# Two stages of row-wise work in a graph network: table rows added by TensorE, small layer-norm operations for pairs of groups

## The chip, the cores and the metric

The kernel runs on one core of one Trainium2 chip, in fp32. The metric is the device time of one execution in microseconds. Three executions of the kernel before took 2436.28, 2438.08 and 2440.83 us (median 2438.08).

## The reference

50000 nodes have 160 features, 64 scalars and 32 vectors of 3; 25000 edges join them. Two layers of message passing are computed, each followed by a residual and a layer norm over the 160 features of a node:

```python
x = _layernorm(x + _L0_gnn_ref(x, node_vec1, src, dst, edge_attr_4, edge_attr_64, ...))
x = _layernorm(x + _L1_gnn_ref(x, node_vec1, edge_attr_16, edge_attr_4, src, dst, ...))
```

What the first layer does with a node, once the messages of its edges have been summed and mapped (`o_s`, `o_v`), is this:

```python
pre_s = sc_s + o_s          # sc_s = s @ sc_ws * a * inv : the self-connection, 96 columns
pre_v = sc_v + o_v          # sc_v : the same for the vectors, 3 x 32 columns
scalars = silu(pre_s[:, :64])
gates = sigmoid(pre_s[:, 64:96])
gated = gates[:, :, None] * pre_v
```

The layer norm is `(x - mean) / sqrt(var + 1e-5)`.

## The kernel before

The work has four stages, one after the other: edges of layer 0, nodes of layer 0, edges of layer 1, nodes of layer 1. The two edge stages run over 98 pairs of 128-edge tiles (gather rows of the source nodes, compute messages, sum those with the same destination, scatter-add them to a table in HBM). The two node stages run over NG = 98 groups of T = 4 tiles of 128 nodes. The change lies in the node stages.

Every engine has its own instruction stream, written out by hand. `run_stages` (L56) writes a software pipeline: in its step k an engine runs a list of pairs (lag, function), each function for group k - lag, in the order of the list. Buffers are rings of four (index u = g mod 4) or of two. Engines meet only in semaphores that count groups; `wait_count(engine, semaphore, n)` waits for a count of n, and engines execute in order, so that whatever stands behind a wait waits too. In functions, g is the count of groups from which the counts of the waits are made (it goes on from 98 in the second node stage).

The first node stage does this with group g:

- SP loads the turned features (`load_turned`, L374, two DMAs `xT` and `zT`) and the rows of the summed messages (`load_table`, L387, tile `tab`, 384 KB).
- TensorE: `nodes0` (L608) multiplies the features with the self-connection's weights into PSUM (`n0_ps`, two buffers; L603 for four tiles of 160 columns, L605 for the rest); `turn_back` (L614) turns the features back into rows in PSUM (`x0_ps`, `z0_ps`) for the residual.
- DVE: `add_table` (L896) adds PSUM and the table's rows into `tab`, which frees the PSUM buffer.
- ACT: `gates` (L715) takes the sigmoid of the first 96 columns, in four instructions.
- GpSimd: `scale_gates` (L499) multiplies them with the node's attribute.
- DVE: `gated0` (L903), two products into `res` (ring of four; it waits until group g - 4 has been normalised, `s_y`); `residual0` (L911), two additions from PSUM; `stats_of` (L947), four `bn_stats`.
- GpSimd: `powers` (L463) makes `rstd` and `shift` of the group from the statistics: eleven instructions on 128 x 4 elements with waits for its own results between them, `pow` at L483.
- ACT: `normalise` (L738), four activations of 160 columns with scale and bias per partition into `y`; `store` (L747) issues the DMA to HBM.

The order in a step of each engine, before:

```python
# TensorE                                                      L642
run_stages(pe, 0, NG, 6, [(0, nodes0), (1, turn_back)])
# ACT                                                          L755
[(0, gates)] ... + [(5, store), (4, normalise)]
# GpSimd                                                       L506
run_stages(pool, 0, NG, 10, [(0, scale_gates), (3, powers)])
# DVE                                                          L956
run_stages(dve, 0, NG, 6, [(2, gated0), (0, add_table), (2, residual0), (3, stats_of)])
```

The second node stage has the same tail: GpSimd runs `factor` (L487, three small operations for a group's mean over edges) and `powers` with lag 1 (L508); DVE runs `residual1` (L918), `stats_of` with lag 1 and `table_row1` (L939, which needs `factor`'s result) (L958); TensorE turns the features (`turn1`) and multiplies (`nodes1`) through `self_connection` (L600), which both stages share; ACT copies from PSUM and normalises as in the first (L755).

## Time and profile before

| what | value |
| --- | --- |
| median of 3 runs | 2438.08 us |
| runs | 2436.28 to 2440.83 us |
| profiled execution: span from first to last instruction | 2446.7 us |
| profiled execution: its own timer | not shown |
| PE / DVE / ACT / GpSimd busy, share of span | 71% / 62% / 44% / 72% |
| first node stage (L901, first to last start) | 867.5 to 1280.4 us |
| second node stage (L944, first to last start) | 2024.2 to 2434.8 us |
| TensorE's mean granted clock | 0.837 |

The span is that of one profiled execution, the times are of others. PE is TensorE, POOL GpSimd, SP the engine that issues loads; PEld is TensorE's loading of weights, which overlaps its matmuls. The granted clock is a share of 2.4 GHz: 0.5 is the lower level, 1.2 GHz. Each fp32 matmul of the code stands in the trace as two records, each transpose as one. In a timeline a row with xN is N instructions of one line that follow each other, from the start of the first to the end of the last; the ends of matmuls are modelled.

### The profile page before, as it was taken

To read this page: it belongs to the slowest core of one execution; us is meant where nothing else is said; L and a number is where in the kernel's file an instruction comes from. 1 tells how busy PE (TensorE), PEld (TensorE's weight loads), DVE (VectorE), ACT (ScalarE), POOL (GpSimd) and SP (SyncE) were. 2 spreads that over 40 slices of the span, in tenths; PEclk is the share of its full clock that TensorE was granted. 3 is DMA by queue.
4 is the path that set the end of the run, shared out by engine and by line. 5 is a ranking of instruction groups with operands and counts; after the bars stand their busy time and mean duration, and the time that the engine had idled before them with its cause. 6 is when DMAs were issued, how large, how long until landed. Compare 5 with 4: busy or idle time off the path is not lost. (4 is left out here: it accounts for less than half of the span.)

```text
span 2446.7 us, 50266 instructions
## 1 busy us (share of the span) xinstructions
PE 1726.5 (71%) x10412; PEld 1528.8 (62%) x10412; DVE 1506.3 (62%) x6121; ACT 1070.8 (44%) x3336; POOL 1751.4 (72%) x3148
## 2 busy tenths in 40 slices
PE   0478888888888666666665878678777766666664
PEld 0367776777776566666664767567666655556564
DVE  1266666666666468888883444444444427888886
ACT  0233333333333246666663333333333325566665
POOL 1066677766667568888884777777777757888887
PEclk9988889888888788888875888988798878878877
DMA  5975555555555467777772444444444436666664
GB/s 223 422 198 121 117 117 117 119 117 116 118 118 119 77 202 252 240 244 243 240 221 69 71 67 69 70 70 69 69 68 69 70 53 226 234 232 235 230 236 175
DMA packets 270387, 374.52 MB, mean 153 GB/s; under 512 B 62544, under 2 KB 172944, under 8 KB 267280
## 3 DMA queue, kind: packets, MB, share of 16 engines
q1 hardware_dynamic: 163264, 203.38, 28.8%
q0 software_dynamic: 75264, 67.79, 19.3%
q10 hardware_dynamic: 31824, 102.97, 10.4%
q8 instruction: 11, 0.18, 0.0%
q14 instruction: 24, 0.20, 0.0%
HBM read 202.83 MB, written 171.16 MB: 153 GB/s over the span
## 5 line engine op out<-in xcount | busy, mean ns | idle before, releaser
L453 POOL DMA_INDIRECT table<-sums,row_i x392 | 632.9, 1615 | 307.0 <-ACT sums L710 104.1
L743 ACT ACTIVATE y<-res,shift,rstd 128x160 f32<-128x160 f32 x784 | 343.8, 509 | 307.4 <-POOL shift L485 307.3
L695 ACT COPY msg<-ps 128x192 f32<-128x192 f32 (+1 forms) x196 | 57.4, 293 | 620.3 <-PE ps L592 437.1
L438 POOL DMA_INDIRECT xg<-in_x_rows,src_i x196 | 199.3, 1017 | 172.2 <-DMA src_i<-in_src_col 69.7
L603 PE MATMUL ps<-self_m,xT 128*128 128x160 f32 (+1 forms) x1568 | 303.8, 350 | 7.6 <-DVE tab L901 4.6
L526 PE MATMUL ps<-ident,xg 128*128 128x128 f32 x392 | 94.1, 325 | 293.1 <-ACT xz L682 214.8
L603 PEld LDWEIGHTS ps<-self_m,xT 128*128 128x128 f32 x1568 | 266.7, 239 | 17.2 <-issue 5.3
L526 PEld LDWEIGHTS ps<-ident,xg 128*128 128x128 f32 x392 | 42.3, 151 | 353.6 <-ACT xz L682 194.4
L438 POOL DMA_INDIRECT xg<-x_rows,src_i x196 | 195.5, 997 | 70.8 <-issue 62.9
L573 PE MATMUL ps<-mapA,midT 128*128 128x128 f32 (+1 forms) x784 | 189.1, 329 | 50.3 <-DVE msg L848 47.8
L483 POOL TENSOR_TENSOR rstd<-var_e,minus_half 128x4 f32<-128x4 f32 x196 | 203.7, 1039 | 15.4
L952 DVE BATCH_NORM_STATS2 stats<-res 128x6 f32<-128x160 f32 x784 | 194.8, 308 | 6.1 <-POOL shift L485 6.0
L573 PEld LDWEIGHTS ps<-mapA,midT 128*128 128x128 f32 x784 | 145.2, 231 | 72.1 <-issue 64.4
L807 DVE TENSOR_TENSOR prod<-hs,ea_all 128x192 f32<-128x192 f32 x196 | 70.2, 358 | 184.5 <-ACT hs L670 163.3
L575 PE MATMUL ps<-mapB,midT 128*128 128x96 f32 x784 | 177.4, 315 | 0.0
L627 PE MATMUL ps<-ident,x1g 128*128 128x128 f32 x392 | 74.9, 322 | 141.6 <-ACT x1z L729 133.7
L618 PE MATMUL ps<-ident,xT 128*128 128x128 f32 x392 | 73.7, 317 | 139.1 <-DVE res L916 138.9
L944 DVE SCALAR_TENSOR_TENSOR res<-tab,small,res 128x160 f32<-128x160 f32 x392 | 124.6, 379 | 69.8 <-POOL small L497 69.7
L886 DVE COPY row_i<-row_all 128x2 int32 (+1 forms) x98 | 17.5, 178 | 237.0 <-DMA table<-sums,row_i 234.9
L559 PE MATMUL ps<-ident,mid 128*128 128x128 f32 x784 | 154.9, 334 | 0.0
L575 PEld LDWEIGHTS ps<-mapB,midT 128*128 128x128 f32 x784 | 150.2, 238 | 0.0
L627 PEld LDWEIGHTS ps<-ident,x1g 128*128 128x128 f32 x392 | 48.5, 160 | 156.9 <-ACT x1z L729 105.6
(121 smaller groups left out, 5019.8 us busy)
## 6 DMA issues: line engine op xcount, KB each, us to landing
...
dst_row<-in_dst_row SPq DMA_DIRECT2D x196, 128.0 KB
```

What stands on the lines that cost most here:

```text
L438: pool.indirect_dma_start(out=xg[u][:, t, 0:width], out_offset=None, in_=rows, in_offset=bass.IndirectOffsetOnAxis(ap=src_i[u][:, t:t + 1] ...
L453: pool.indirect_dma_start(out=table[l], out_offset=bass.IndirectOffsetOnAxis(ap=row_i[u][:, t:t + 1], axis=0), in_=sums[u][:, t, 0:W], in_ ...
L483: tt(rstd[u][:, :], var_e[:, :], minus_half[:, :], ALU.pow).then_inc(s_rstd, 1)
L526: turn(xgT_ps[:, t, :], xg[u][:, t, 0:M], ident[:, :])
L559: last = turn(midT_ps[:, 2 * c + t, :], mid[u][:, t, c * P:(c + 1) * P], ident[:, :])
L573: mm(o_ps[l][:, t, 0:SO + V], midT[u][:, t, :], mapA[l][:, :], start=t == 0, stop=not L["cross"], skip_group_check=True)
L575: last = mm(o_ps[l][:, t, SO + V:SO + 4 * V], midT[u][:, 2 + t, :], mapB[l][:, :], start=False, stop=not L["cross"], skip_group_check=True)
L603: mm(o[:, t // 2, t % 2, 0:z], xT[u][:, t * P:(t + 1) * P], w_m[:, :], start=True, stop=True)
L627: turn(x1T_ps[u][:, t * P:(t + 1) * P], x1g[u][:, t, 0:M], ident[:, :])
L743: last = nc.scalar.activation(y[u][:, t, :], res[u][:, t, :], ACT.Identity, scale=rstd[u][:, t:t + 1], bias=shift[u][:, t:t + 1])
L944: last = stt(res[u][:, t, :], tab1[u][:, t, 1:161], small[u][:, t, 3:4], res[u][:, t, :], ALU.mult, ALU.add)
L952: last = nc.vector.bn_stats(stats[u][:, t, :], res[u][:, t, :])
```

## The change

In the first node stage TensorE adds the table's rows: `nodes0` accumulates identity times `tab` (four matmuls of 192 columns) on top of the self-connection in PSUM, and `add_table` is gone. ACT's sigmoid and DVE's products read PSUM in place of `tab`, and `nodes0` waits for `s_f` (the products of group g - 2) in place of `s_added`. The turned features come in one DMA into one tile; the z part is turned back by two transposes into the same PSUM rows as x, and the residual is one addition. `load_table` is released by `s_np`. DVE's order in a step and its lags change, TensorE's too.

In both node stages `powers` runs for two groups at once, when the second has its statistics, on 128 x 8 elements (ten instructions; no product with 0.25, a doubling of rstd in its place), and the fourth tile of each group is normalised by GpSimd (`normalise_last`), which `store` and the next user of `res` wait for (`s_y3`).

```diff
...
-xT = four("xT", [M, GROUP])
-zT = four("zT", [T * V, P])
+xzT = four("xzT", [P, GROUP + P])
+xT = [w[0:M, 0:GROUP] for w in xzT]
+zT = [w[0:T * V, GROUP:GROUP + P] for w in xzT]
 x1g = four("x1g", [P, T, D])
 x1z = two("x1z", [P, T, V])
 tab = four("tab", [P, T, 192])
 gate = two("gate", [P, T, 96])
 res = four("res", [P, T, D])
-stats = two("stats", [P, T, 6])
-mean2, apart, squares, apart2, var_in, var_e, neg_mean = [
-    sb(n, [P, T]) for n in ("mean2", "apart", "squares", "apart2", "var_in", "var_e", "neg_mean")]
-rstd = four("rstd", [P, T])
-shift = four("shift", [P, T])
+stats2 = [sb(f"stats{h}", [P, 2, T, 6]) for h in range(2)]
+stats = [stats2[u // 2][:, u % 2, :, :] for u in range(4)]
+mean2, apart, squares, apart2, var_in, var4, neg_mean2, half_rstd = [
+    sb(n, [P, 2 * T]) for n in ("mean2", "apart", "squares", "apart2", "var_in", "var4", "neg_mean2", "half_rstd")]
+rstd2 = [sb(f"rstd{h}", [P, 2 * T]) for h in range(2)]
+shift2 = [sb(f"shift{h}", [P, 2 * T]) for h in range(2)]
+rstd = [rstd2[u // 2][:, u % 2 * T:(u % 2 + 1) * T] for u in range(4)]
+shift = [shift2[u // 2][:, u % 2 * T:(u % 2 + 1) * T] for u in range(4)]
...
-n0_ps = [ps[:, u * 1024:(u + 1) * 1024].rearrange("p (b c) -> p b c", b=2)[:, :, 0:384]
-         .rearrange("p b (t c) -> p b t c", t=2) for u in range(2)]
-x0_ps = [bank(4 + 2 * u).rearrange("p (t c) -> p t c", t=T) for u in range(2)]
-z0_ps = [bank(5 + 2 * u, T * V).rearrange("p (t c) -> p t c", t=T) for u in range(2)]
-x1T_ps = [bank(2 * u) for u in range(2)]
-z1T_ps = [bank(2 * u + 1, P) for u in range(2)]
-n1_ps = [ps[:, (2 + u) * 1024:(3 + u) * 1024].rearrange("p (b c) -> p b c", b=2)[:, :, 0:2 * D]
-         .rearrange("p b (t c) -> p b t c", t=2) for u in range(2)]
-n0_ps, x0_ps, z0_ps, x1T_ps, z1T_ps, n1_ps = [b * 2 for b in (n0_ps, x0_ps, z0_ps, x1T_ps, z1T_ps, n1_ps)]
+def rows_of(b, n):
+    return ps[:, b * 512:(b + 2) * 512].rearrange("p (t c) -> p t c", t=T)[:, :, 0:n]
+n0_ps = [rows_of(2 * u, 192) for u in range(2)] * 2
+x0_ps = [rows_of(4 + 2 * u, D) for u in range(2)] * 2
+x1T_ps = [bank(2 * u) for u in range(2)] * 2
+z1T_ps = [bank(2 * u + 1, P) for u in range(2)] * 2
+n1_ps = [rows_of(4 + 2 * u, D) for u in range(2)] * 2
...
         def load_turned(g, m, u):
...
-            sp.dma_start(xT[u][:, :], A["xT"][bass.ds(m, 1)].rearrange("a k n -> k (a n)")).then_inc(s_nxT[u], 16)
-            sp.dma_start(zT[u][:, :], A["zT"][bass.ds(m, 1)].rearrange("a k n -> k (a n)")).then_inc(s_nxT[u], 16)
+            sp.dma_start(xzT[u][:, :], A["xzT"][bass.ds(m, 1)].rearrange("a k n -> k (a n)")).then_inc(s_nxT[u], 32)
         def load_x1(g, m, u):
...
-            wait_count(sp, s_res, g - 3)
+            wait_count(sp, s_res if l else s_np, g - 3)
...
         def powers(g, m, u):
-            st = stats[u]
+            if u % 2 == 0:
+                return
+            h = u // 2
+            st = stats2[h][:, :, :, :].rearrange("p g t s -> p (g t) s")
             tt, ts = nc.gpsimd.tensor_tensor, nc.gpsimd.tensor_scalar
             pool.wait_ge(s_bn, g + 1)
             wait_count(pool, s_y, g - 3)
-            tt(mean2[:, :], st[:, :, 1], st[:, :, 4], ALU.add)
             tt(apart[:, :], st[:, :, 1], st[:, :, 4], ALU.subtract)
-            tt(squares[:, :], st[:, :, 2], st[:, :, 5], ALU.add).then_inc(s_p1, 1)
+            tt(squares[:, :], st[:, :, 2], st[:, :, 5], ALU.add)
+            tt(mean2[:, :], st[:, :, 1], st[:, :, 4], ALU.add).then_inc(s_p1, 2)
             pool.wait_ge(s_p1, g + 1)
             tt(apart2[:, :], apart[:, :], apart[:, :], ALU.mult)
-            ts(neg_mean[:, :], mean2[:, :], -0.5, None, ALU.mult)
-            ts(var_in[:, :], squares[:, :], 1.0 / D, EPS, ALU.mult, ALU.add).then_inc(s_p2, 1)
+            ts(var_in[:, :], squares[:, :], 4.0 / D, 4.0 * EPS, ALU.mult, ALU.add).then_inc(s_p2, 2)
+            ts(neg_mean2[:, :], mean2[:, :], -1.0, None, ALU.mult)
             pool.wait_ge(s_p2, g + 1)
-            tt(apart2[:, :], apart2[:, :], quarter[:, :], ALU.mult).then_inc(s_p3, 1)
+            tt(var4[:, :], var_in[:, :], apart2[:, :], ALU.add).then_inc(s_p3, 2)
             pool.wait_ge(s_p3, g + 1)
-            tt(var_e[:, :], var_in[:, :], apart2[:, :], ALU.add).then_inc(s_p4, 1)
-            pool.wait_ge(s_p4, g + 1)
-            tt(rstd[u][:, :], var_e[:, :], minus_half[:, :], ALU.pow).then_inc(s_rstd, 1)
+            tt(half_rstd[:, :], var4[:, :], minus_half[:, :], ALU.pow).then_inc(s_rstd, 2)
             pool.wait_ge(s_rstd, g + 1)
-            tt(shift[u][:, :], neg_mean[:, :], rstd[u][:, :], ALU.mult).then_inc(s_shift, 1)
+            tt(shift2[h][:, :], neg_mean2[:, :], half_rstd[:, :], ALU.mult)
+            ts(rstd2[h][:, :], half_rstd[:, :], 2.0, None, ALU.mult).then_inc(s_shift, 2)
+        def normalise_last(g, m, u):
+            pool.wait_ge(s_shift, g + 1)
+            wait_count(pool, s_store[u], landed(g - 4, u, 4))
+            pool.sem_inc(s_ntick, 1)
+            nc.gpsimd.tensor_scalar(y[u][:, T - 1, :], res[u][:, T - 1, :], rstd[u][:, T - 1:T], shift[u][:, T - 1:T],
+                                    ALU.mult, ALU.add).then_inc(s_y3, 1)
         def factor(g, m, u):
...
-            run_stages(pool, 0, NG, 10, [(0, scale_gates), (3, powers)])
+            run_stages(pool, 0, NG, 10, [(0, scale_gates), (3, powers), (4, normalise_last)])
         else:
-            run_stages(pool, NG, NG, 6, [(0, factor), (1, powers)])
+            run_stages(pool, NG, NG, 6, [(0, factor), (1, powers), (2, normalise_last)])
...
-        def self_connection(o, z, u, w_m, w_z):
+        def nodes0(g, m, u):
+            pe.wait_ge(s_nxT[u], landed(g, u, 4, 32))
+            wait_count(pe, s_f, g - 1)
+            o = n0_ps[u]
             for t in range(T):
-                mm(o[:, t // 2, t % 2, 0:z], xT[u][:, t * P:(t + 1) * P], w_m[:, :], start=True, stop=True)
+                mm(o[:, t, 0:160], xT[u][:, t * P:(t + 1) * P], self_m[0][:, :], start=t % 2 == 0, stop=False,
+                   skip_group_check=True)
             for b in range(2):
-                last = mm(o[:, b, :, z:z + V], zT[u][:, :], w_z[:, b * 2 * V:(b + 1) * 2 * V], start=True, stop=True)
+                mm(o[:, 2 * b:2 * b + 2, 160:192], zT[u][:, :], self_z[0][:, b * 2 * V:(b + 1) * 2 * V],
+                   start=False, stop=False, skip_group_check=True)
+            pe.wait_ge(s_nx[u], landed(g, u, 4))
+            for t in range(T):
+                last = mm(o[:, t, :], ident[:, :], tab[u][:, t, :], start=False, stop=True, skip_group_check=True)
             last.then_inc(s_np, 1)
-        def nodes0(g, m, u):
-            pe.wait_ge(s_nxT[u], landed(g, u, 4, 32))
-            wait_count(pe, s_added, g - 1)
-            self_connection(n0_ps[u], 160, u, self_m[0], self_z[0])
         def turn_back(g, m, u):
             wait_count(pe, s_res, g - 1)
             for t in range(T):
-                turn(x0_ps[u][:, t, :], xT[u][:, t * P:(t + 1) * P], ident[:, :])
-            turn(z0_ps[u].rearrange("p t c -> p (t c)"), zT[u][:, :], ident[:, :]).then_inc(s_xb, 1)
+                turn(x0_ps[u][:, t, 0:M], xT[u][:, t * P:(t + 1) * P], ident[:, :])
+            for b in range(2):
+                q = slice(b * 2 * V, (b + 1) * 2 * V)
+                last = turn(x0_ps[u][:, 2 * b:2 * b + 2, M:D], zT[u][q, :], ident[q, q])
+            last.then_inc(s_xb, 1)
         def turn1(g, m, u):
...
-            self_connection(n1_ps[u], M, u, self_m[1], self_z[1])
+            o = n1_ps[u]
+            for t in range(T):
+                mm(o[:, t, 0:M], xT[u][:, t * P:(t + 1) * P], self_m[1][:, :], start=True, stop=True)
+            for b in range(2):
+                last = mm(o[:, 2 * b:2 * b + 2, M:D], zT[u][:, :], self_z[1][:, b * 2 * V:(b + 1) * 2 * V],
+                          start=True, stop=True)
+            last.then_inc(s_np, 1)
         pe.wait_ge(s_sumsb, (l + 1) * NP)
         for _ in range(WARM[l]):
             mm(ps[:, 0:512], ident[:, :], zeros[:, 0:512], start=True, stop=True)
         if l == 0:
-            run_stages(pe, 0, NG, 6, [(0, nodes0), (1, turn_back)])
+            run_stages(pe, 0, NG, 6, [(1, turn_back), (0, nodes0)])
...
         def gates(g, m, u):
-            act.wait_ge(s_added, g + 1)
+            act.wait_ge(s_np, g + 1)
             wait_count(act, s_f, g - 1)
             for t in range(T):
                 a = a_all[:, bass.ds(m, 1), t:t + 1].rearrange("p g t -> p (g t)")
-                last = nc.scalar.activation(gate[u][:, t, :], tab[u][:, t, 0:96], ACT.Sigmoid, scale=a)
+                last = nc.scalar.activation(gate[u][:, t, :], n0_ps[u][:, t, 0:96], ACT.Sigmoid, scale=a)
...
-            for t in range(T):
+            for t in range(T - 1):
...
         def store(g, m, u):
...
+            act.wait_ge(s_y3, g + 1)
...
-        def add_table(g, m, u):
-            dve.wait_ge(s_np, g + 1)
-            dve.wait_ge(s_nx[u], landed(g, u, 4))
-            t4 = tab[u][:, :, :].rearrange("p (b t) c -> p b t c", b=2)
-            tt(t4, n0_ps[u], t4, ALU.add).then_inc(s_added, 1)
         def gated0(g, m, u):
             dve.wait_ge(s_scgate, g + 1)
             wait_count(dve, s_y, g - 3)
-            tt(res[u][:, :, 0:S], tab[u][:, :, 0:S], gate[u][:, :, 0:S], ALU.mult)
-            tt(planes(res[u][:, :, S:D]), planes(tab[u][:, :, 96:192]),
+            wait_count(dve, s_y3, g - 3)
+            tt(res[u][:, :, 0:S], n0_ps[u][:, :, 0:S], gate[u][:, :, 0:S], ALU.mult)
+            tt(planes(res[u][:, :, S:D]), planes(n0_ps[u][:, :, 96:192]),
                gate[u][:, :, S:96].unsqueeze(2).to_broadcast([P, T, 3, V]), ALU.mult).then_inc(s_f, 1)
         def residual0(g, m, u):
             dve.wait_ge(s_f, g + 1)
             dve.wait_ge(s_xb, g + 1)
-            tt(res[u][:, :, 0:M], res[u][:, :, 0:M], x0_ps[u], ALU.add)
-            tt(res[u][:, :, M:D], res[u][:, :, M:D], z0_ps[u], ALU.add).then_inc(s_res, 1)
+            tt(res[u][:, :, :], res[u][:, :, :], x0_ps[u], ALU.add).then_inc(s_res, 1)
         def residual1(g, m, u):
...
+            wait_count(dve, s_y3, g - 3)
             def self_connection(t):
                 a = a_all[:, bass.ds(m, 1), t:t + 1].rearrange("p g t -> p (g t)")
-                return stt(res[u][:, t, :], n1_ps[u][:, t // 2, t % 2, :], a, x1g[u][:, t, :], ALU.mult, ALU.add)
+                return stt(res[u][:, t, :], n1_ps[u][:, t, :], a, x1g[u][:, t, :], ALU.mult, ALU.add)
...
         def stats_of(g, m, u):
...
-            wait_count(dve, s_shift, g - 1)
+            wait_count(dve, s_shift, g - 2 - u % 2)
             for t in range(T):
                 last = nc.vector.bn_stats(stats[u][:, t, :], res[u][:, t, :])
             last.then_inc(s_bn, 1)
         if l == 0:
-            run_stages(dve, 0, NG, 6, [(2, gated0), (0, add_table), (2, residual0), (3, stats_of)])
+            run_stages(dve, 0, NG, 6, [(1, gated0), (2, stats_of), (1, residual0)])
...
```

## Rows read from the trace of the kernel before

**Rows 1.** One line of the kernel, L901 (DVE table add), first and last start.
```profile
L901 DVE TENSOR_TENSOR tab<-ps,tab x98: 944/951/959, 867.5 to 1280.4; 128x768 f32<-128x768 f32 x98
```

**Rows 2.** One line, L944 (DVE, second node stage), first and last start.
```profile
L944 DVE SCALAR_TENSOR_TENSOR res<-tab,small,res x392: 366/378/386, 2024.2 to 2434.8; 128x160 f32<-128x160 f32 x196
```

**Rows 3.** Windows: stretch, its us, busy us (instructions) per engine, PEclk, DMA share, GB/s.
```profile
870.00:1270.00 400.00, 266.17 (x1597) 252.10 (x1596) 326.92 (x834) 257.20 (x731) 346.86 (x997) 0.83 0.77 241
...
2030.00:2430.00 400.00, 259.72 (x1593) 237.40 (x1593) 330.91 (x1323) 243.57 (x660) 336.46 (x1230) 0.80 0.67 231
```

**Rows 4.** Waits in 900 to 1260 us: who waited for whom, total, times, longest.
```profile
ACT y L743 <- POOL shift L485: 121.0, 82, 2.0
DVE res L907 <- ACT y L743: 52.1, 72, 0.9
```

**Rows 5.** Timeline, first node stage: start, us, engine, line, operation, count, idle before.
```profile
1049.64 1.81 PE L603 MATMUL ps<-self_m,xT 128*128 128x160 f32 x6
...
1056.36 0.20 POOL L485 TENSOR_TENSOR shift<-neg_mean,rstd 128x4 f32<-128x4 f32 x1
...
1056.55 0.83 POOL L503 TENSOR_TENSOR gate<-gate,a_all 128x384 f32<-128x384 f32 x1
...
1056.69 1.76 ACT L743 ACTIVATE y<-res,shift,rstd 128x160 f32<-128x160 f32 x4 [1.52 <-POOL shift L485]
...
1057.33 0.20 POOL L470 TENSOR_TENSOR mean<-stats 128x4 f32<-128x4 f32 x1
1057.43 1.25 PE L603 MATMUL ps<-self_m,xT 128*128 128x160 f32 x8
...
1058.35 0.62 ACT L722 ACTIVATE gate<-tab,a_all 128x96 f32<-128x96 f32 x2
...
1058.48 0.43 DVE L907 TENSOR_TENSOR res<-tab,gate 128x256 f32<-128x256 f32 x1 [0.80 <-ACT y L743]
1058.52 0.55 PE L605 MATMUL ps<-self_z,zT 128*128 128x64 f32 x4
...
1058.82 0.55 DVE L908 TENSOR_TENSOR res<-tab,gate 128x384 f32<-128x384 f32 x1
...
1058.88 0.63 ACT L722 ACTIVATE gate<-tab,a_all 128x96 f32<-128x96 f32 x2
```

**Rows 6.** Timeline, last group's small operations on GpSimd, undisturbed.
```profile
2437.16 0.20 POOL L470 TENSOR_TENSOR mean<-stats 128x4 f32<-128x4 f32 x1
...
2437.75 0.20 POOL L474 TENSOR_TENSOR apart<-apart 128x4 f32<-128x4 f32 x1
2437.91 0.23 POOL L475 TENSOR_SCALAR neg_mean<-mean 128x4 f32<-128x4 f32 x1
2438.20 0.19 POOL L476 TENSOR_SCALAR var_in<-squares 128x4 f32<-128x4 f32 x1
...
2439.03 1.04 POOL L483 TENSOR_TENSOR rstd<-var_e,minus_half 128x4 f32<-128x4 f32 x1
...
2440.14 0.20 POOL L485 TENSOR_TENSOR shift<-neg_mean,rstd 128x4 f32<-128x4 f32 x1
```

**Rows 7.** Groups by line, GpSimd only, whole run.
```profile
L425 POOL CAST spare_row<-spare_i 128x196 f32<-128x196 int32 x1 | 0.3, 338 | 0.0
```

**Rows 8.** Waits in 2060 to 2420 us, second node stage.
```profile
DVE res L944 <- POOL small L497: 61.9, 85, 0.9
```

**Rows 9.** Timeline, second node stage.
```profile
2200.93 0.20 POOL L497 TENSOR_TENSOR small<-small 128x4 f32<-128x4 f32 x1
...
2201.25 1.27 DVE L944 SCALAR_TENSOR_TENSOR res<-tab,small,res 128x160 f32<-128x160 f32 x4 [0.92 <-POOL small L497]
...
2201.95 0.36 POOL L475 TENSOR_SCALAR neg_mean<-mean 128x4 f32<-128x4 f32 x1
...
2202.44 0.18 DVE L923 TENSOR_SCALAR small<-tab 128x4 f32<-128x4 f32 x1
...
2203.76 0.99 DVE L952 BATCH_NORM_STATS2 stats<-res 128x6 f32<-128x160 f32 x4
```

17 lines of the change are left out of this document (8 added, 9 removed).

## The prediction

> **What bounds the kernel now.** I first placed the two node stages: L901 runs once a group, 98 times from 867.5 to 1280.4 us [rows 1], so a group of the first node stage takes 412.9/97 = 4.26 us; L944 gives 410.6/391 x 4 = 4.20 us for the second [rows 2]. The windows then show what is full in them [rows 3]: GpSimd is busy 346.9 of 400 us in the first and 336.5 in the second, DVE 82%, TensorE 67% and 65%, ACT 64% and 61%. The waits say the same: ACT's normalisation waits 121 us for the shift that GpSimd makes, DVE's gating waits 52 us for that normalisation [rows 4], and in the second stage DVE waits 61.9 us for GpSimd's factor [rows 8]. GpSimd's short idle stretches are its waits on its own results: L470 to L474 takes 0.59 us for three 0.15 us steps and a wait [rows 6]. So GpSimd bounds both stages, with a loop that is its own instruction stream. Nothing in the edge stages or in the weights is touched; I cost them at nothing.
>
> **The change, part by part.** A group is g, a step of an engine's loop is k; k is even below.
>
> *Small operations for a pair (W).* Now nine instructions and six waits per group; after, ten instructions once per two groups, so they cost W once per pair. From the undisturbed run [rows 6], by starts: three sums and their wait 0.59; L474 to L475 0.16; a tensor-scalar step (L475 to L476) 0.29; L476 to L483 is three steps in 0.83, so 0.28 each, and the new order has two of them before the power: 0.56; the power and its wait, L483 to L485, 1.11; shift 0.16; the added doubling of rstd, by L475, 0.23 to its end. W = 3.10 us if the power costs the same for 8 elements a partition as for 4. Its price at 8 is in no row. It lies between nothing more and twice its excess over a plain operation (1.04 - 0.20 = 0.84 us), that is W = 3.10 to 3.94. The nearest row on elements is the cast of 196 elements at 338 ns [rows 7] against 200 ns for 4, which shows that GpSimd's time grows with elements; an excess of 0.84 us that only the power has reads as work per element. I take 3.94. The Trainium skill, GPSIMD Engine Reference, section 2.1, describes an elementwise instruction as a loop over the elements in each core; by it the power doubles, W = 3.94; the other reading would give 3.10.
>
> *Fourth tile on GpSimd.* One tensor-scalar of 160 elements: between 0.23 (4 elements [rows 6]) and 0.83 (384 elements, two inputs [rows 5]); nearest is the cast, 0.34 for 196 [rows 7]; with two operands per partition to read I take 0.45, plus 0.08 wait. It takes a quarter off ACT: four activations start 1056.69, the next work starts at 1058.35 [rows 5], so 0.415 each; three take 1.76 - 0.415 = 1.345 us.
>
> *Table rows on TensorE.* L901's 0.95 us leaves DVE. TensorE gets eight more records a group (each fp32 matmul of this kernel has two) of 192 columns. Eight of 160 columns take 1057.43 to 1058.52 = 1.09 us at full clock [rows 5], so 192 columns cost 1.09 x 192/160 = 1.31 us. nodes0 then lasts 1.09 + 0.55 + 1.31 = 2.95 us. At 1.2 GHz six records took 1.81 us [rows 5], twice as slow, so up to 2.7 us more. The splitting of the z transpose adds one record of about 0.15 us that is on no loop.
>
> *Residual in one DVE operation* saves some 0.14 us of DVE; not on a loop. *One load for x and z* takes one issue from SP, whose queue ends nothing here: nothing. The table row's load must now have landed for TensorE instead of for DVE, and is issued on an earlier release (self-connection done, not residual): nothing while it runs three groups ahead.
>
> *The new waits are the main term.* Two edges meet. First, powers run only for odd g, at GpSimd's step g+3. ACT's normalise(k-4), k even, is in step k, and its shift now comes from powers(k-3) in GpSimd's same step k, behind scale_gates(k); before, it had come one step earlier. Second, the gating reads PSUM itself, so nodes0(k+2) waits until gated0(k) has freed the one of two buffers; before, the table add freed it. And gated0(k) waits, as before, for normalise(k-4), whose row buffer it overwrites. That closes a loop over two groups: gates(k), scale_gates(k), powers(k-3), normalise(k-4), gated0(k), nodes0(k+2), gates(k+2). By pieces [rows 5]: gates to GpSimd about 0.10 (the handovers in these rows are 0.03 to 0.13); scale to next start 1056.55 to 1057.33 = 0.78; W; shift end 1056.56 to y start 1056.69 = 0.13; three tiles 1.345; y to gating 0.06; gating 1058.48 to 1059.37 = 0.89; to TensorE 0.10; nodes0 2.95; to ACT 0.10; gates 1058.35 to 1059.51 = 1.16. Without W: 7.62. The pair takes 11.56 us (W 3.94) or 10.72 (W 3.10) at full clock, 5.78 or 5.36 a group. Nothing hides in it: behind the waiting normalise(k-4) on ACT stand gates(k+1) and the store; behind gated0(k) on DVE the statistics and the residual; behind nodes0(k+2) on TensorE all that follows.
>
> The clock: the window shows a granted mean of 0.83 [rows 3], so it is at the lower level (0.5) for 0.17/0.5 = 34% of the time. TensorE's busy share in the new loop is about like now (some 7 of 11.6 us), so I keep 34%: 0.34 x 2.7 = 0.9 us a pair. That gives 12.5/2 = 6.23 us a group, and 98 x (6.23 - 4.26) = +193 us. Bounds: no low clock and W 3.10: 98 x 1.10 = +108; always low and W 3.94: 14.26/2 = 7.13, +281. TensorE's idle time will come in one piece of 3 to 4 us a pair instead of about 2 us a group; the Trainium skill, TensorE: Matmul & The Clock Gate, section "HAM oscillation", says that idle stretches bring the lower clock back; by it the sum would lie nearer the upper bound.
>
> *Second node stage.* There the pair also queues factor(g+2) behind powers(g) and normalise_last. Loop over two groups: statistics end, 0.10, W (stretched some 0.15: L475 takes 0.36 beside DVE's L944 [rows 9] against 0.23), last tile 0.53, factor three small steps 0.76, 0.12 to L944, L944 to L923 1.19, L923 to L952 1.32, L952 0.99 [rows 9]: 5.16 + W = 9.10 or 8.26, 4.55 or 4.13 a group: 98 x (4.55 - 4.20) = +34 us, or -7.
>
> *Sum.* +193 + 34 = +227 us (with W 3.10: +152 - 7 = +145). The profiled execution spans 2446.7 us, 8.6 us above the median of 2438.08; its own timer is not shown. The sum is made against its rows: 2446.7 + 227 = 2673.7, less 8.6, is 2665 us.
>
> **Rivals.** (A) The forecast, W 3.94: 2665; 0.47. (B) Same loop, the power costs as much for a pair as for one: 2438 + 145 = 2583; for it, that a batch is cheap on every other operation; against it the excess above; 0.22. (C) Same loop, clock low throughout: 2438 + 281 + 34 = 2753; for it the longer idle piece, against it that TensorE is 60% busy; 0.11. (D) nodes0 is hidden after all, and the loop of ACT and GpSimd alone is left (0.10 + 0.78 + W + 0.13 + 2 x 1.245 + 1.06 + 1.16 = 5.72 + W, 4.41 to 4.83 a group): +15 to +56 in the first stage, 2446 to 2528 in all; it needs gated0(k) not to wait for normalise(k-4), against the text of the waits; 0.09. (E) Faster: GpSimd's relief counts and no loop closes. Its load falls to (1.76 + W + 1.06)/2 = 2.96 to 3.38 a group, and TensorE is next. It decides at the row buffer: if normalise(k-4) is done when scale_gates(k) is, gated0 never waits. TensorE has 266.2/400 x 4.26 = 2.83 us a group at clock 0.83, 2.35 at full, plus 1.31 = 3.66: 98 x (3.66 - 4.26) = -59, with -7: 2372; 0.08. (F) The same with TensorE's clock still 0.83: 3.66/0.83 = 4.41, +15 - 7: within what is told from no change or a little over; 0.03, of which I count 0.02 as the same.
>
> **The numbers.** Slower is A, B, C, D and the rest of F: 0.90; same 0.02; faster 0.08. A measurement of this kernel tells about 0.2% (5 us) from no change. The range takes in A and B with the bounds of the clock and of the last tile, and leaves out E, F, most of D and most of C: 2530 to 2725 us.
>
> **What the profile of after would show.** Right: nodes0 matmuls come in two bursts and then a gap of 3 to 4 us, every 11 to 12.5 us; TensorE waits for DVE's gating, DVE's gating for ACT's y, ACT's y for GpSimd's shift, ACT's gates for TensorE, in turn; GpSimd busy below 70% in that stage. The power's duration at 128x8 decides between A (1.9 us) and B (1.04 us). Granted clock in the stage decides C. Wrong: a group of the first stage below 4.9 us, TensorE busy over 90% there, or GpSimd still without waits for others. For the second stage: DVE's L944 waits for GpSimd in every other group, about 1 us longer than now.

## The result and the profile after

The changed kernel takes 2855.45 us (median of 4 runs, 2847.37 to 2864.11) where the kernel before took 2439.45 us (4 runs, 2436.28 to 2445.26) beside it: a ratio of 1.170, 95% interval 1.168 to 1.173. It is slower by 416 us. The forecast was slower, 2665 us, at most 2725.

The head of the page of after (the profiled execution's span, then each engine's busy time):

```profile
span 2862.3 us, 51071 instructions
...
PE 1942.3 (68%) x11294; PEld 1745.8 (61%) x11294; DVE 1408.2 (49%) x5925; ACT 973.1 (34%) x3140; POOL 1610.2 (56%) x2363
```

Every engine but TensorE has less to do than before, and the span is 415.6 us longer: the time is in waits. The stages are measured on one line each, by first and last start. GpSimd's scaling of the gates, once a group, in the first node stage:

```profile
L499 POOL TENSOR_TENSOR gate<-gate,a_all x98: 827/827/829, 881.9 to 1532.9; 128x384 f32<-128x384 f32 x98
```

DVE's L945 in the second, four times a group (it answers to [rows 2]):

```profile
L945 DVE SCALAR_TENSOR_TENSOR res<-tab,small,res x392: 362/374/522, 2264.1 to 2849.4; 128x160 f32<-128x160 f32 x196
```

That is (1532.9 - 881.9)/97 = 6.71 us a group in the first stage, and (2849.4 - 2264.1)/391 x 4 = 5.99 in the second. Before, the same lines give 4.30 and 4.20. (The forecast took 4.26 for the first stage, from L901, which starts 2.2 us before the gates' scaling and ends 5.9 us before it.) So the first stage gained 98 x 2.41 = 237 us and the second 98 x 1.79 = 175 us; together 412 of the 415.6. The windows of both stages, with the columns of [rows 3] (PE, PEld, DVE, ACT, POOL, then clock, DMA share, GB/s):

```profile
900.00:1500.00 600.00, 414.82 (x2282) 389.30 (x2282) 218.49 (x616) 198.90 (x616) 262.43 (x613) 0.80 0.45 153
...
2270.00:2840.00 570.00, 279.57 (x1582) 273.33 (x1583) 333.92 (x1312) 199.41 (x563) 273.93 (x844) 0.70 0.47 162
```

GpSimd, 87% and 84% busy before, is at 44% and 48%. The mean granted clock of TensorE is 0.80 in the first stage (0.83 before) and 0.70 in the second (0.80 before).

### The profile page after: what moved, and what is told of

Same layout as the page of the kernel before. It is cut to its first block and busy times, and to the rows that moved or that the text cites. A ratio compares the mean times of both kernels' runs of the same rounds, so it can differ in the third digit from the quotient of the medians.

```text
span 2862.3 us, 51071 instructions
## 1 busy us (share of the span) xinstructions
PE 1942.3 (68%) x11294; PEld 1745.8 (61%) x11294; DVE 1408.2 (49%) x5925; ACT 973.1 (34%) x3140; POOL 1610.2 (56%) x2363
## 5 line engine op out<-in xcount | busy, mean ns | idle before, releaser
L749 ACT ACTIVATE y<-res,shift,rstd 128x160 f32<-128x160 f32 x588 | 263.2, 513 | 626.3 <-POOL rstd L474 624.1
L602 PE MATMUL ps<-self_m,xzT 128*128 128x160 f32 x784 | 169.3, 371 | 193.6 <-DVE res L909 193.6
L628 PE MATMUL ps<-ident,x1g 128*128 128x128 f32 x392 | 96.9, 396 | 293.7 <-ACT x1z L735 283.4
L499 POOL TENSOR_TENSOR gate<-gate,a_all 128x384 f32<-128x384 f32 x98 | 81.1, 827 | 341.2 <-ACT gate L728 341.2
L602 PEld LDWEIGHTS ps<-self_m,xzT 128*128 128x128 f32 x784 | 138.6, 232 | 204.0 <-DVE res L909 200.0
L628 PEld LDWEIGHTS ps<-ident,x1g 128*128 128x128 f32 x392 | 70.8, 218 | 300.7 <-ACT x1z L735 289.7
L908 DVE TENSOR_TENSOR res<-ps,gate 128x256 f32<-128x256 f32 x98 | 41.4, 423 | 431.7 <-ACT y L749 406.7
L609 PE MATMUL ps<-tab,ident 128*128 128x192 f32 x784 | 192.8, 402 | 5.3 <-DMA tab<-table 5.3
L953 DVE BATCH_NORM_STATS2 stats<-res 128x6 f32<-128x160 f32 x784 | 194.6, 309 | 0.1
L945 DVE SCALAR_TENSOR_TENSOR res<-tab,small,res 128x160 f32<-128x160 f32 x392 | 129.9, 391 | 121.8 <-POOL small L493 121.6
L931 DVE SCALAR_TENSOR_TENSOR res<-ps,a_all,x1g 128x160 f32<-128x160 f32 x392 | 128.7, 368 | 117.2 <-PE ps L639 117.2
L728 ACT ACTIVATE gate<-ps,a_all 128x96 f32<-128x96 f32 x392 | 100.1, 335 | 219.4 <-PE ps L609 219.4
L609 PEld LDWEIGHTS ps<-tab,ident 128*128 128x128 f32 x784 | 170.9, 248 | 5.5 <-DMA tab<-table 5.5
```

The costliest lines, as they stand in the source:

```text
L602: mm(o[:, t, 0:160], xT[u][:, t * P:(t + 1) * P], self_m[0][:, :], start=t % 2 == 0, stop=False, skip_group_check=True)
L609: last = mm(o[:, t, :], ident[:, :], tab[u][:, t, :], start=False, stop=True, skip_group_check=True)
L628: turn(x1T_ps[u][:, t * P:(t + 1) * P], x1g[u][:, t, 0:M], ident[:, :])
L749: last = nc.scalar.activation(y[u][:, t, :], res[u][:, t, :], ACT.Identity, scale=rstd[u][:, t:t + 1], bias=shift[u][:, t:t + 1])
L931: return stt(res[u][:, t, :], n1_ps[u][:, t, :], a, x1g[u][:, t, :], ALU.mult, ALU.add)
L945: last = stt(res[u][:, t, :], tab1[u][:, t, 1:161], small[u][:, t, 3:4], res[u][:, t, :], ALU.mult, ALU.add)
```

## Reading the two loops

The waits of the first stage, who waited for whom, total us, times, longest:

```profile
DVE res L908 <- ACT y L749: 380.4, 44, 9.1
...
ACT y L749 <- POOL rstd L474: 218.9, 44, 5.0
...
PE ps L602 <- DVE res L909: 185.2, 44, 4.3
ACT gate L728 <- PE ps L609: 183.4, 44, 4.6
```

Each of DVE, TensorE, ACT (for the shift) and ACT (for the gates) waits 44 times in 88 groups, once a pair, and each for the next one of the chain. The timeline shows one turn of it:

```profile
1101.96 0.35 ACT L728 ACTIVATE gate<-ps,a_all 128x96 f32<-128x96 f32 x1
1102.50 0.83 POOL L499 TENSOR_TENSOR gate<-gate,a_all 128x384 f32<-128x384 f32 x1 [5.48 <-ACT gate L728]
...
1103.28 0.21 POOL L461 TENSOR_TENSOR apart<-stats 128x8 f32<-128x8 f32 x1
...
1105.01 1.67 POOL L471 TENSOR_TENSOR half_rstd<-var,minus_half 128x8 f32<-128x8 f32 x1
...
1106.92 0.24 POOL L474 TENSOR_SCALAR rstd<-half_rstd 128x8 f32<-128x8 f32 x1
1107.30 1.34 ACT L749 ACTIVATE y<-res,shift,rstd 128x160 f32<-128x160 f32 x3 [4.99 <-POOL rstd L474]
...
1108.67 0.42 DVE L908 TENSOR_TENSOR res<-ps,gate 128x256 f32<-128x256 f32 x1 [9.00 <-ACT y L749]
...
1109.01 0.55 DVE L909 TENSOR_TENSOR res<-ps,gate 128x384 f32<-128x384 f32 x1
...
1109.61 1.15 PEld L602 LDWEIGHTS ps<-self_m,xzT 128*128 128x128 f32 x8 [4.38 <-DVE res L909]
...
1111.70 2.68 PE L609 MATMUL ps<-tab,ident 128*128 128x192 f32 x8
...
1114.52 0.81 ACT L728 ACTIVATE gate<-ps,a_all 128x96 f32<-128x96 f32 x3 [3.74 <-PE ps L609]
...
1115.21 0.35 ACT L728 ACTIVATE gate<-ps,a_all 128x96 f32<-128x96 f32 x1
```

Here as in the forecast, k is even and a turn is two groups. The gates of an even group end at 1102.31. Then, each piece from the end of the one before: 0.19 to the scaling's start, 0.78 to L461, 3.88 for the pair's small operations (L461 to the end of L474), 0.14, 1.34 for ACT's three tiles, 0.03, 0.89 for the gating (to 1109.56), 0.05, 4.77 for TensorE's nodes0 (L602 to the end of L609), 0.14, 1.04 for the next gates. The sum is 13.25 us, 8.48 of it without nodes0. The 46 full turns of the stage take 13.2 to 14.0 us, 13.66 on the mean; the stage's 2 x 6.71 = 13.42 has its first and last groups in it, where the loop is not closed. What varies is nodes0: in the 42 turns between 900 and 1500 us in which it can be read whole, it took 4.76 to 5.53 us, 5.14 on the mean, which leaves 8.52 for the rest. The forecast had 8.61 and 3.87.

The waits of the second stage:

```profile
ACT y L749 <- POOL rstd L474: 371.5, 47, 8.0
...
PE ps L628 <- ACT x1z L735: 283.4, 46, 6.7
POOL small L489 <- DVE small L935: 197.8, 46, 4.5
...
DVE res L931 <- PE ps L639: 114.8, 46, 2.7
```

Here too each is counted once a pair, but TensorE's wait for `x1z` and DVE's wait for `nodes1` are on a way that the forecast did not follow. One turn:

```profile
2404.62 0.21 POOL L461 TENSOR_TENSOR apart<-stats 128x8 f32<-128x8 f32 x1 [0.96 <-DVE stats L953]
...
2408.54 0.24 POOL L474 TENSOR_SCALAR rstd<-half_rstd 128x8 f32<-128x8 f32 x1
2408.91 1.34 ACT L749 ACTIVATE y<-res,shift,rstd 128x160 f32<-128x160 f32 x3 [7.96 <-POOL rstd L474]
...
2410.16 0.28 ACT L735 COPY x1z<-x1g 128x128 f32<-128x128 f32 x1
...
2410.49 0.71 PEld L628 LDWEIGHTS ps<-ident,x1g 128*128 128x128 f32 x4 [5.59 <-ACT x1z L735]
...
2411.61 1.91 PE L637 MATMUL ps<-self_m,xzT 128*128 128x128 f32 x8
...
2413.32 0.95 PE L639 MATMUL ps<-self_z,xzT 128*128 128x64 f32 x4
...
2414.60 0.38 DVE L931 SCALAR_TENSOR_TENSOR res<-ps,a_all,x1g 128x160 f32<-128x160 f32 x1 [2.70 <-PE ps L639]
...
2415.85 0.99 DVE L953 BATCH_NORM_STATS2 stats<-res 128x6 f32<-128x160 f32 x4
...
2417.00 0.21 POOL L461 TENSOR_TENSOR apart<-stats 128x8 f32<-128x8 f32 x1 [0.94 <-DVE stats L953]
```

Powers (L461 to the end of L474) 4.16 us; 0.13; ACT normalises the even group, and 1.25 us after its start comes `copy_z1`, which had stood behind the waiting normalisation in ACT's queue; 0.33 to `turn1` (L628); 1.12 to `nodes1` (L637), which stands behind it on TensorE; 2.66 for it, at the lower clock; 0.33; `residual1` 1.25; the statistics 0.99; 0.16 to the next pair's powers. The sum is 12.38 us. The 47 full turns take 11.65 to 12.38, 12.16 on the mean; the stage's 2 x 5.99 = 11.98 again has its ends in it.

## The experiments

All are compared by the two measures above, us a group in the first and second stage; the kernel before is 4.30 and 4.20, the changed one 6.71 and 5.99. The kernel before took 2448 to 2457 us beside them, some 10 us more than beside the changed kernel, so totals are read to about 10 us and stages to a few hundredths.

**1. The row buffer, the edge that closes the first loop.**

```diff
+gf = two("gf", [P, T, D])
 # gated0
-wait_count(dve, s_y, g - 3)
-wait_count(dve, s_y3, g - 3)
-tt(res[u][:, :, 0:S], ...)
+wait_count(dve, s_res, g - 1)
+tt(gf[u][:, :, 0:S], ...)
 # residual0
+wait_count(dve, s_y, g - 3)
+wait_count(dve, s_y3, g - 3)
-tt(res[u][:, :, :], res[u][:, :, :], x0_ps[u], ALU.add)
+tt(res[u][:, :, :], gf[u][:, :, :], x0_ps[u], ALU.add)
```

> The changed kernel, with the gated rows in a ring of two of their own, so that gated0 no longer waits for the normalisation of group g - 4; residual0 does. Only that edge of the first stage's loop is cut. Theory L (a loop over two groups through powers, normalise, gated0, nodes0 and gates sets the first stage): it falls from 6.71 us a group to 4.7 to 5.0, what the loop of ACT and GpSimd leaves (gates to scale 0.19, 0.78, powers 3.88, 0.14, normalise 1.24, gates 0.90, normalise 1.24, gates 1.04 = 9.41 a pair), so 168 to 197 us less, 2660 to 2690 us in all; the second stage stays at 5.99. Rival P (TensorE's eight added records and its low clock set the stage by their length): no more than 20 us less.

Measured: 2668.5 us, 4.70 and 5.98. Scaling of the gates in this run:

```profile
L500 POOL TENSOR_TENSOR gate<-gate,a_all x98: 825/827/829, 870.8 to 1326.3; 128x384 f32<-128x384 f32 x98
```

(1326.3 - 870.8)/97 = 4.70, where the remaining loop of ACT and GpSimd sums to 9.41 a pair, 4.71 a group. TensorE does the same work as in the changed kernel, and the stage is 2.0 us a group shorter: the loop is shown, and TensorE's added records as a cause by their length are ruled out.

**2. ACT's queue in the second stage.**

```diff
-[(5, store), (4, normalise)]
+[(5, store), (4, normalise)] if l == 0 else [(6, store), (5, normalise)]
```

> The changed kernel, with ACT's normalise at lag 5 and store at lag 6 in the second node stage alone, so that copy_z1 and copy_nT of the next step stand ahead of the normalisation that waits for a pair's shift. Theory Q (in the second stage the waiting normalise holds up ACT's queue, and with it TensorE's turn1 and nodes1, DVE's residual1 and the statistics of the next pair): 5.99 us a group falls to 4.2 to 4.6, 136 to 175 us less, 2680 to 2720 us; granted clock there back to about 0.8. Rival C (TensorE's lower clock, 0.70 for 0.80, or the length of the pair's powers is the cause by itself): within 25 us of 2855. The first stage is not touched.

Measured: 2738.3 us, 6.71 and 4.73. DVE's L945 in this run:

```profile
L945 DVE SCALAR_TENSOR_TENSOR res<-tab,small,res x392: 358/372/521, 2260.9 to 2723.7; 128x160 f32<-128x160 f32 x196
```

A reordering of two queue entries takes 1.25 us a group, 123 us, out of the stage; granted clock is 0.75 there (2300 to 2600 us). That is less than the 1.4 to 1.8 expected, and what is left is the loop that the forecast had as the stage's only one:

```profile
2405.49 0.24 POOL L474 TENSOR_SCALAR rstd<-half_rstd 128x8 f32<-128x8 f32 x1
...
2406.03 0.48 POOL L480 TENSOR_SCALAR y<-res,rstd,shift 128x160 f32<-128x160 f32 x1 [0.30 <-POOL rstd L474]
2406.47 0.21 POOL L489 TENSOR_TENSOR small<-a_all,small 128x4 f32<-128x4 f32 x1
...
2407.36 1.40 DVE L945 SCALAR_TENSOR_TENSOR res<-tab,small,res 128x160 f32<-128x160 f32 x4 [2.52 <-POOL small L493]
...
2408.68 0.16 DVE L923 TENSOR_SCALAR small<-tab 128x4 f32<-128x4 f32 x1
...
2409.99 0.99 DVE L953 BATCH_NORM_STATS2 stats<-res 128x6 f32<-128x160 f32 x4
```

Powers' end, last tile (L480), factor (L489), `table_row1` (L945), `residual1` from L923, statistics (L953), next powers: forecast 9.10 us a pair, measured 2 x 4.73 = 9.47.

**3. The small operations for one group again.** `powers` and its tiles as in the kernel before; the rest as changed.

```diff
 # powers
-if u % 2 == 0:
-    return
-st = stats2[h][:, :, :, :].rearrange("p g t s -> p (g t) s")
+st = stats[u]
...
 # stats_of
-wait_count(dve, s_shift, g - 2 - u % 2)
+wait_count(dve, s_shift, g - 1)
```

> The changed kernel with the small operations per group again, as before the change; TensorE's table add, the one residual operation and the fourth tile on GpSimd stay. Theory L and Q: both loops are over two groups because of the pair; without it GpSimd is full and bounds both stages: 3.4 + 0.88 + 0.53 = 4.8 us a group in the first, 4.20 + 0.53 = 4.75 in the second, so 2855 - 98 x (1.91 + 1.24) = 2546 us. Rival P (TensorE's table add and the PSUM buffer held until gated0 set the first stage): first stage above 5.5, second 4.75, 2620 us or more.

Measured: 2568.6 us, 5.05 and 4.65. The pair is thus worth 1.66 and 1.34 us a group, 294 us of the loss in the setting of the changed kernel. The first stage is 0.25 above the 4.8 that I had summed for GpSimd. The wait there, in 1000 to 1300 us:

```profile
DVE res L906 <- POOL y L478: 151.8, 58, 4.9
```

DVE's gating waits, once a group, for the fourth tile on GpSimd, not for ACT. That led to a theory of its own, tested in the next run.

**4. TensorE's table add without pair and without fourth tile.** The one residual operation, the one load and the new orders of DVE and TensorE stay with it.

```diff
 # on the kernel of experiment 3
-run_stages(pool, 0, NG, 10, [(0, scale_gates), (3, powers), (4, normalise_last)])
+run_stages(pool, 0, NG, 10, [(0, scale_gates), (3, powers)])
-run_stages(pool, NG, NG, 6, [(0, factor), (1, powers), (2, normalise_last)])
+run_stages(pool, NG, NG, 6, [(0, factor), (1, powers)])
 # normalise, on ACT
-for t in range(T - 1):
+for t in range(T):
```

> The changed kernel with the small operations per group and all four tiles normalised by ACT: of the change TensorE's table add, the one residual operation, the one load and the orders of DVE and TensorE are left. In the run with single operations DVE's gating waited for the fourth tile on GpSimd, which stands behind the small operations there. Theory F (the fourth tile on GpSimd closes a loop of its own in the first stage): it falls from 5.05 to GpSimd's own load of 4.3 us a group, the second stage from 4.65 to 4.2, 2445 to 2465 us in all. Rival P (TensorE's table add with the PSUM buffer held until gated0 is what is left): first stage 4.8 or more, 2490 us or more.

Measured: 2423.8 us, 4.01 and 4.20; ratio to the kernel before 0.988 (0.980 to 0.996; 2 runs against 3). Without the fourth tile the first stage loses 1.04 us and the second 0.44. More than expected: this part of the change alone is a gain, 0.28 us a group under the kernel before, though GpSimd has the same instructions. Two of them show it, in 1000 to 1250 us of the kernel before and then of this one (busy, mean ns | idle before):

```profile
L481 POOL TENSOR_TENSOR var_e<-var_in,apart 128x4 f32<-128x4 f32 x58 | 19.9, 344 | 4.5
L479 POOL TENSOR_TENSOR apart<-apart,quarter 128x4 f32<-128x4 f32 x58 | 18.6, 320 | 4.8
```

```profile
L466 POOL TENSOR_TENSOR apart<-apart,quarter 128x4 f32<-128x4 f32 x63 | 12.6, 200 | 5.3
L468 POOL TENSOR_TENSOR var_e<-var_in,apart 128x4 f32<-128x4 f32 x63 | 12.6, 200 | 4.9
```

The sum and the product took 344 and 320 ns on the mean, and take 200 now; that is 0.26 of the 0.28 us. In the kernel before they ran beside DVE's gating, which read `tab` and `gate`, both in SBUF; now DVE reads PSUM and `gate`. Two turns of the kernel before tell the gating from DVE's other work:

```profile
1050.73 0.20 POOL L481 TENSOR_TENSOR var_e<-var_in,apart 128x4 f32<-128x4 f32 x1
...
1059.04 0.39 POOL L481 TENSOR_TENSOR var_e<-var_in,apart 128x4 f32<-128x4 f32 x1
```

The first ran beside the table add (one input in PSUM), the second beside the gating (L908, from 1058.82). The Trainium skill, SBUF — State Buffer, section "Who interferes with whom", states this: a DVE instruction with two SBUF inputs contends with a GpSimd instruction that reads SBUF, one with at most one SBUF input does not. This trace agrees: 0.39 us against 0.20. A window of the stage:

```profile
1000.00:1250.00 250.00, 237.35 (x1617) 208.69 (x1615) 162.52 (x436) 173.67 (x500) 218.03 (x685) 1.00 0.78 262
```

TensorE is busy 95% of it, and its clock is granted in full, 1.00 against 0.83 before.

**5. The pair alone, on the kernel before.** `powers` for two groups with its tiles, and the statistics' wait that belongs to it; nothing else.

```diff
 # powers
+if u % 2 == 0:
+    return
-st = stats[u]
+st = stats2[h][:, :, :, :].rearrange("p g t s -> p (g t) s")
...
 # stats_of
-wait_count(dve, s_shift, g - 1)
+wait_count(dve, s_shift, g - 2 - u % 2)
```

> The kernel before with nothing but the small operations of two groups at once. Theory L: the loop closes without TensorE's table add too, but shorter, by way of DVE's add_table (which stands behind gated0 on DVE) in place of nodes0: 0.19 + 0.78 + 3.88 + 0.14 + 1.76 + 0.06 + 0.89 + 0.95 + 0.1 + 1.16 = 9.9 a pair, 4.95 a group, +68 us. Theory Q: the second stage goes to 6.0 or a little more (four tiles to normalise), +175 to +200. In all 2680 to 2710 us. Rival P: the pair by itself only relieves GpSimd, and this kernel is faster than before (2438), by up to 60 us.

Measured: 2740.5 us, 5.29 and 6.15. The pair costs without TensorE's part and without the fourth tile; in the second stage, where the change has little but pair and fourth tile, it is all of the loss (6.15 against 5.99). In the first stage 0.34 us a group is missing in my sum (4.95); granted clock there is 0.77 (900 to 1250 us), and I did not follow it up.

**6. The clock, first try.** The changed kernel, with twelve matmuls more in `turn_back` of odd groups, ahead of the last two transposes:

```diff
+if u % 2:
+    for _ in range(12):
+        mm(ps[:, 3232:3328], ident[:, :], ident[:, 0:96], start=True, stop=True)
```

> The changed kernel with twelve matmuls of 96 columns more in turn_back of every second group, into PSUM columns that nobody reads, in the 4.2 us in which TensorE waits for the gating. In the profile of after the nodes0 on the loop takes about 4.95 us a pair on the mean, against 3.10 at full clock. Theory K (the idle time brings the lower clock, and that is the 1.1 us a pair that my sum lacked): granted clock in the first stage from 0.80 to over 0.95, nodes0 near 3.1, 60 to 90 us less in the first stage, 2765 to 2795 us. Rival: the filler only delays nodes0, or the clock is lowered by the load itself: within 15 us of 2855 or above. The second stage is not touched.

Measured: 2812.9 us, 6.26 and 5.98: 44 us less in the first stage, where 60 to 90 were expected. TensorE's timeline:

```profile
1108.41 2.82 PE L619 MATMUL ps<-ident 128*128 128x96 f32 x24
...
1113.02 1.90 PE L602 MATMUL ps<-self_m,xzT 128*128 128x160 f32 x8 [1.58 <-DVE res L912]
```

There is still 1.58 us without work, and in this turn nodes0 is slow. Windows of half a microsecond (us, busy, clock, DMA share, GB/s) show that the clock was at the upper level while TensorE idled, and fell to 1.2 GHz within a microsecond of nodes0's start:

```profile
1112.50:1113.00 0.50, 0.00 (x0) 1.00 0.87 128
...
1114.00:1114.50 0.50, 0.50 (x4) 0.50 0.87 207
```

Not so in every turn. Of 41 turns between 900 and 1440 us nodes0 took 4.66 to 4.77 us in 24 and 3.10 us in 17, after the same 1.56 to 1.60 us of idle time but for the first three. So the length of the idle time does not by itself decide whether the clock falls.

**7. The length of the pair's operations.** This run leaves out the reciprocal square root: a product of constants stands in for the power.

```diff
-tt(half_rstd[:, :], var4[:, :], minus_half[:, :], ALU.pow)
+tt(half_rstd[:, :], minus_half[:, :], minus_half[:, :], ALU.mult)
```

> The changed kernel with the power replaced by a product of constants, 1.67 us to about 0.2: it leaves out the reciprocal square root. Theory L and Q (the small operations lie whole on both loops over a pair): 1.47 us less a pair in each stage, 49 x 2 x 1.47 = 144 us less, 2711 us. Rival P or C (TensorE sets the stages): less than 40 us gained.

Measured: 2639.8 us, 5.24 and 5.25, 216 us less. In the second stage the pair is 2 x (5.99 - 5.25) = 1.48 us shorter, what the product saves (1.667 - 0.202 = 1.47). In the first it is 2.95 us shorter, twice that: TensorE idles 2.7 us a pair in place of 4.2, the granted clock rises to 0.96 (1000 to 1250 us), and nodes0 took 3.10 us in 37 of 44 turns. The small operations lie whole on both loops, and in the first stage the time that they lost here was gained once more by way of the clock.

**8. Slack restored.** `gf` as in 1; no tile on GpSimd; pair in the first stage alone, with `normalise` at lag 5 there; in the second stage the small operations per group, in the form of the change, and a later group's shift to wait for in the statistics (`g - 3`, with statistics in a ring of four). That form has as many instructions as the one before, ten (the forecast counted nine before, the description of the kernel eleven; the profile of before shows ten), but waits for an own result once less: the product with 0.25 is gone, and the doubling in its place waits for nothing new.

```diff
 # ACT
-[(5, store), (4, normalise)]
+[(6, store), (5, normalise)] if l == 0 else [(5, store), (4, normalise)]
 # GpSimd; powers1 is the pair's powers on one group's [P, T]
-[(0, scale_gates), (3, powers), (4, normalise_last)]
+[(0, scale_gates), (3, powers)]
-[(0, factor), (1, powers), (2, normalise_last)]
+[(0, factor), (1, powers1)]
```

> The changed kernel with both loops cut: gated rows in a ring of their own, normalise at lag 5 in the first stage, no tile on GpSimd, pairs in the first stage alone; in the second stage the small operations per group in the ten-instruction form. Theory L, Q and F: no loop is left over one pair; the first stage is set by TensorE's work (3.66 us at full clock) or GpSimd's (0.88 + 1.95 = 2.9): 3.8 to 4.1 us a group; the second by GpSimd, 4.05 to 4.15: 2390 to 2425 us, below the kernel before. Rival P: TensorE's work or clock holds the first stage at 4.4 or more: 2440 us or more.

Measured: 2418.2 us, 4.13 and 3.99; ratio 0.986 (0.979 to 0.992). The first stage, with less GpSimd work than in 4, is still slower than there (4.01): in this arrangement the pair gives nothing even with slack. What bounds it now I did not follow to the end. GpSimd is busy 61% of 1000 to 1250 us; DVE's residual waits 96.6 us there for ACT's y, once a group, and TensorE for that residual 30 times, once a pair, so a pattern over two groups is left. In the second stage the form of the change and the later wait together give 0.21 us a group.

**9. The clock, second try.** As 6, with eighteen matmuls.

```diff
-    for _ in range(12):
+    for _ in range(18):
```

> As the run with twelve filler matmuls, with eighteen. With twelve TensorE still idled 1.57 us before nodes0 and the clock fell 0.5 us after nodes0 had begun. Theory K: with the idle time nearly gone the clock stays at the upper level, nodes0 takes 3.1 us in place of 4.95 on the loop: 11.6 us a pair, 5.8 us a group, 2765 us in all. Rival (the low stretch comes whatever TensorE does before): 6.26 us a group as with twelve, 2810 us, or more.

Measured: 2774.5 us, 5.83 and 5.98. TensorE's timeline:

```profile
1105.32 4.16 PE L619 MATMUL ps<-ident 128*128 128x96 f32 x36
...
1109.90 1.35 PE L602 MATMUL ps<-self_m,xzT 128*128 128x160 f32 x8 [0.21 <-DVE res L912]
```

The idle time is down to 0.21 us, the granted clock of 1000 to 1250 us is 1.00, nodes0 takes 3.10 us in every turn, and the loop 2 x 5.83 = 11.66 against 8.52 + 3.10 = 11.62. The clock is shown as the term by which the first stage exceeded its sum: 49 x 4.16 = 204 us of matmuls whose results nobody reads make the kernel 81 us faster.

**10. The version that beats both.** The kernel of 4, with the small operations of each group in the form of the change in both stages, and the later wait of the statistics.

```diff
 # powers, for each group, on [P, T]
+tt(ap, st[:, :, 1], st[:, :, 4], ALU.subtract)
+tt(sq, st[:, :, 2], st[:, :, 5], ALU.add)
+tt(m2, st[:, :, 1], st[:, :, 4], ALU.add).then_inc(s_p1, 1)
...
+ts(vi, sq, 4.0 / D, 4.0 * EPS, ALU.mult, ALU.add).then_inc(s_p2, 1)
+ts(nm, m2, -1.0, None, ALU.mult)
...
+ts(rstd[u], hr, 2.0, None, ALU.mult).then_inc(s_shift, 1)
 # stats_of
-wait_count(dve, s_shift, g - 1)
+wait_count(dve, s_shift, g - 3)
```

> The table add alone (the run with 4.01 and 4.20 us a group), with the small operations of one group in the ten-instruction form in both stages, which gave 3.99 in the second stage of the run with slack restored. GpSimd bounds both stages: 3.8 to 3.9 us a group in the first (TensorE's 3.66 is near), 3.99 in the second: 2424 - 98 x (0.15 + 0.21) = 2388 us, range 2380 to 2400, ratio to the kernel before 0.973 to 0.983. If TensorE bounds the first stage at 4.0 already, 2403 us.

Measured: 2385.15 us (5 runs, 2382.93 to 2392.74) against 2453.47 of the kernel before beside it (9 runs): ratio 0.9735, 0.9712 to 0.9759. 3.87 and 3.98 us a group. GpSimd is busy 224.6 of 250 us in the first stage (1000 to 1250 us) and 152.4 of 180 in the second (2200 to 2380), and has no wait for another engine in either; the rest is its waits on itself. What the form and what the later wait give apart was not tried.

**11. The pair without the fourth tile.** The changed kernel with four tiles on ACT; the waits for the fourth tile go too.

```diff
-[(0, scale_gates), (3, powers), (4, normalise_last)]
+[(0, scale_gates), (3, powers)]
-[(0, factor), (1, powers), (2, normalise_last)]
+[(0, factor), (1, powers)]
-for t in range(T - 1):
+for t in range(T):
```

> The changed kernel with all four tiles normalised by ACT, pairs kept. Theory L and Q: ACT's normalisation of the even group lies on both loops, a fourth tile costs 0.415 us a pair in each: 6.92 and 6.20 us a group, 2855 + 98 x 0.42 = 2896 us. Rival F (the fourth tile on GpSimd costs as it does with single operations, 1.04 and 0.44 us a group): 2710 to 2800 us.

Measured: 2870.8 us, 6.73 and 6.15. The second stage is 0.16 longer for 0.21 expected. In the first only 0.02 of 0.21 is seen; the tile costs 0.41 us a pair on the loop, but the granted clock is 0.87 (900 to 1500 us) for 0.80, and nodes0 takes 4.75 us on the mean of 42 turns for 5.14. Why the clock is better here, after 4.6 us of idle time for 4.2, is open. With the pair the fourth tile on GpSimd is a small gain, without the pair (3 against 4) a loss of 145 us in all.

## Why the prediction was right and wrong

**What bounded the kernel before**: right. GpSimd, in both stages, with its own stream; experiment 4 moved the first stage by 0.28 us, 0.26 of it in the durations of two GpSimd operations, and 10 moved both by taking one wait for an own result out of GpSimd's stream.

**The pair's length**: right within 0.06 us by luck, from two errors that offset each other. The power at 8 elements:

```profile
L471 POOL TENSOR_TENSOR half_rstd<-var,minus_half x98: 1667/1667/1685, 899.7 to 2852.6; 128x8 f32<-128x8 f32 x98
```

It takes 1.667 us where 1.037 was measured for 4, so 0.41 + 0.157 an element: neither the 1.88 of the reading that the work is all per element, nor 1.04. The loop over the elements that the Trainium skill describes (GPSIMD Engine Reference, section 2.1) agrees with the 0.63 us that four elements more cost; the doubling drawn from it does not, since a part is fixed. Waits between the others cost 0.15 us more than I had, and W came to 3.88 for 3.94. The last tile took 0.479 us for my 0.45.

**The loop of the first stage**: right in every edge. The sum without nodes0 was 8.61 at W 3.94 (11.56 less 2.95), measured 8.52. nodes0 at full clock is 3.10 for 2.95. The signs named for this case came too: one gap of 4.2 us a pair, the waits in the order given, GpSimd at 44%; only the turn is longer, 13.66 us for 11 to 12.5. The mis-sized term is the clock, in the sentence "TensorE's busy share in the new loop is about like now, so I keep 34%". The share of low clock over the stage is indeed about that (0.80 for 0.83), but it is not spread evenly: it begins during or soon after the idle time, and after the idle time comes the one nodes0 of each pair that lies on the loop. In the turn shown it began within that nodes0, which had started at 1109.61:

```profile
1110.50:1111.00 0.50, 0.50 (x5) 0.64 0.16 56
```

It lasted until 1114. On the mean nodes0 took 5.14 us, 3.10 plus 2.04, where I had given 0.92 for the low clock. So nodes0 is 1.27 us a pair over its term of 3.87 and everything else 0.09 under its own, 58 us over 49 pairs; with 12 us less for the ends of the stage, where the loop is not closed, and the baseline at 4.30 for 4.26, that makes +235 of the measured +237 us, for +193. By the rule that I had cited from the Trainium skill (TensorE: Matmul & The Clock Gate, section "HAM oscillation"), that idle stretches bring the lower clock back, the sum was to lie nearer the upper bound. The trace agrees in this: nodes0's 5.14 is nearer to the bound's 2.95 + 2.7 = 5.65 than to 3.87. And experiment 9, with the idle time filled, has the clock at 1.00.

**The second stage**: wrong, and most of the miss: +175 for +34. The step that failed is "Loop over two groups: statistics end, W, last tile, factor, ..." as the only loop. It followed the waits of DVE and GpSimd, the engines that were busiest. L945 does wait for GpSimd once a pair (119.1 us in 47 times, 2.5 each), as forecast, but that wait is not the longest way. The longer loop goes by ACT's queue: behind the normalisation that waits for the pair stand `copy_z1` and `copy_nT`, and behind these TensorE's `turn1` and, in its order, `nodes1`, on which `residual1` waits. The rule that I set myself for the first stage (name what is queued behind the waiting instruction, and who waits for that) I did not apply to the second. It took 12.16 us a pair where my loop had 9.10. Experiment 2 cuts just that, and leaves my loop with 9.47 us.

**The fourth tile**: costed at 0.53 us of GpSimd, with no loop of its own. With the pair that holds: by the stages the kernel with it is 18 us faster than without (11). Without the pair it closes one through gating (3 against 4).

**The table add on TensorE**: its side effects stood in no term of the sum. It makes GpSimd's operations beside the gating shorter, and without the pair TensorE is busy 95% of the stage at full clock; with the orders and the one residual operation that belong to it, it is worth 1.2%. What made the change lose is the pair (3, 5).

**Rivals**: C, the same loop with the clock low throughout, was nearest in size (2753), and its mechanism was partly at work: it gave the first stage +281 us, where +237 was measured. What it lacked is the second stage, in which no rival saw a cost over 34 us. E, in which GpSimd's relief counts, needed slack; experiment 8 supplied it, and even then the first stage took 4.13 us a group, where E had 3.66.
